# Half-length filter products in level 0 of a two-level convolution and adapter kernel

## The reference, cut to what matters

```
x = x + ffn0(cond0(x, style))
x = x + ffn1(cond1(x, style))
```

## Time and profile before

| | |
|---|---|
| median of 3 runs | 991.29 us (990.24 to 991.54) |
| profiled execution | 990.33 us, span 988.8 us |
| TensorE (PE) | 940.2 us busy, 95%, 4636 matmuls |
| VectorE (DVE) | 558.3 us, 56% |
| ScalarE (ACT) | 376.2 us, 38% |
| GpSimd (POOL) | 111.0 us, 11% |
| chain that ended last | PE 88%, DVE 8%, issue 2% |

### The profile page before, as it was taken

One profiled execution on the slowest core, in us unless ns is written; L12 is line 12 of the kernel. 1 busy time (PEld: TensorE's weight loads), 2 busy tenths in 40 slices (PEclk: granted clock), 3 DMA queues, 4 the chain that ended last, 5 costly groups with the idle time before them and its releaser, 6 DMA issues.

```text
span 988.8 us, 14065 instructions
## 1 busy us (share of the span) xinstructions
PE 940.2 (95%) x4636; PEld 792.4 (80%) x4636; DVE 558.3 (56%) x1133; ACT 376.2 (38%) x717; POOL 111.0 (11%) x141
## 2 busy tenths in 40 slices
PE   5899999999999999999999998839999999999997
PEld 4777888888888888888888887638888888888886
DVE  8894353353353354344344333966677767777774
ACT  2672243243243243233233221434554445444541
POOL 7100000000000000000000000710112111211121
PEclk8799999999999999999999999859999999999999
DMA  8701011011011011101101101331221222112211
GB/s 281 244 5 65 22 42 64 21 42 64 21 42 64 25 39 64 40 25 63 42 28 57 42 21 54 54 106 29 100 85 64 65 96 94 64 64 87 96 50 64
DMA packets 33567, 64.12 MB, mean 65 GB/s; under 512 B 12304, under 2 KB 13968, under 8 KB 33552
## 3 DMA queue, kind: packets, MB, share of 16 engines
q1 hardware_dynamic: 24480, 30.90, 10.6%
q0 software_dynamic: 9072, 33.03, 9.2%
HBM read 47.14 MB, written 16.78 MB: 65 GB/s over the span
## 4 chain that ended last, share of the span: by engine, by line
PE 88%; DVE 8%; issue 2%; ACT 1%; DMA 1%; POOL 0%; SPq 0%; POOLq 0%; DVEq 0%; ACTq 0%
PE conv_ps L172 9%; PE conv_ps L174 8%; PE conv_ps L173 8%; PE fold_ps L581 6%; PE prod_ps L743 6%; PE prod_ps L744 6%; PE prod_ps L745 6%; PE prod_ps L725 6%; PE prod_ps L726 6%; PE prod_ps L727 6%; PE prod_ps L824 6%; PE prod_ps L823 6%; PE fold_ps L548 3%; PE turn_ps L682 3%; PE turn_ps L704 1%
## 5 line engine op out<-in xcount | busy, mean ns | idle before, releaser
L158 DVE TENSOR_TENSOR h_lo<-conv_ps,h_hi 64x512 fp32r<-64x512 f32 x128 | 88.2, 689 | 47.3 <-ACT h_hi L637 46.4
L172 PE MATMUL conv_ps<-h_hi,e_hi 128*128 128x512 f32 x256 | 104.9, 410 | 2.4 <-issue 2.4
L657 ACT ACTIVATE cond<-conv_ps,bias,demod_tab 128x510 f32<-128x510 f32 x64 | 49.9, 779 | 144.7 <-PE conv_ps L174 132.7
L173 PE MATMUL conv_ps<-h_lo,e_hi 128*128 128x512 f32 x256 | 102.2, 399 | 0.0
L174 PE MATMUL conv_ps<-h_hi,e_lo 128*128 128x512 f32 x256 | 102.1, 399 | 0.0
L743 PE MATMUL prod_ps<-b_hi,xt 128*128 128x512 f32 x256 | 99.9, 390 | 2.3 <-DVE xt L158 2.3
L823 PE MATMUL prod_ps<-quant,xt_hi 128*128 128x512 f32 x256 | 100.3, 392 | 1.4 <-DVE xt_lo L158 1.4
L801 DVE SCALAR_TENSOR_TENSOR res<-prod_ps,norm,res 128x512 f32<-128x512 f32 x32 | 23.9, 750 | 137.3 <-PE prod_ps L745 137.3
L726 PE MATMUL prod_ps<-a_lo,xt 128*128 128x512 f32 x256 | 101.0, 395 | 0.0
L725 PE MATMUL prod_ps<-a_hi,xt 128*128 128x512 f32 x256 | 101.0, 394 | 0.0
L727 PE MATMUL prod_ps<-a_hi,xt 128*128 128x512 f32 x256 | 101.0, 394 | 0.0
(11 more groups left out here) (222 smaller groups left out, 1982.4 us busy)
## 6 DMA issues: line engine op xcount, KB each, us to landing
x_in<-in_x SPq DMA_DIRECT2D x64, 128.0 KB, 2.7
res<-in_x POOLq DMA_DIRECT2D x16, 512.0 KB, 3.6
x_after_first<-res POOLq DMA_DIRECT2D x16, 512.0 KB, 2.9
x_in<-x_after_first SPq DMA_DIRECT2D x64, 128.0 KB, 2.7
res<-x_after_first POOLq DMA_DIRECT2D x16, 512.0 KB, 3.5
out_x<-res POOLq DMA_DIRECT2D x15, 512.0 KB, 2.9
a_raw<-in_adapter_in SPq DMA_DIRECT2D x8, 512.0 KB, 8.1
b_raw<-in_adapter_out SPq DMA_DIRECT2D x8, 512.0 KB, 8.0
```

Source lines behind the costliest of these rows:

```text
L158: return nc.vector.tensor_tensor(out, whole, hi.bitcast(F32), ALU.subtract)
L172: nc.tensor.matmul(out, hi(w), moving_hi(i), start=(i == 0), stop=False)
L173: nc.tensor.matmul(out, hi(w), moving_lo(i), start=False, stop=False)
```

## The change

In level 0 the filter products are made by a scheme with three products of half length in place of four of full length. Layer 1's result is split by column parity into two halves, `CENTRE` and `ODD` (each `T2 = 256` columns, with a pad). VectorE forms differences, `BEFORE = ODD - CENTRE` and `AFTER = ODD (one column on) - CENTRE`; the sums of neighbouring filter tiles are two more tiles (4 and 5). TensorE makes a middle part (sum tiles by `CENTRE`, in `fold_ps[a]`) and two outer parts (in the halves of `conv_ps[a]`), 18 matmuls of 256 columns in all. ScalarE scales the middle; VectorE joins it with both outer parts (`dve_join`); ScalarE writes the two edge columns afterwards (`act_ends`). Level 1 keeps the four products (`pe_second_cond` and its like), but the taps' order is reversed so that layer 1's high and low parts are one 128-partition instruction each.

```
         def act_layer1(act, c, a, bufs):
-            nc.scalar.activation(ps[:, :], ps[:, :], ACT.Identity, bias=..., scale=...).then_inc(S.layer1_scaled, 1)
-            nc.scalar.activation(hi[0:C, 1:H + 1], ps[0:C, :], ACT.Identity)
-            nc.scalar.activation(hi[C:P, 2:H + 2], ps[C:P, :], ACT.Identity).then_inc(S.layer1_hi, 1)
+            for first, parity in ((CENTRE, 0), (ODD + 1, 1)):
+                last = nc.scalar.activation(data[:, first:first + T2], by_parity[:, parity, :], ACT.Identity, bias=..., scale=...)
+            last.then_inc(S.layer1_scaled, 1)
+        def dve_differences(v, c, a, bufs):
+            v.wait_ge(S.layer1_scaled, 2 * c + a + 1)
+            nc.vector.tensor_tensor(data[:, BEFORE:BEFORE + SPAN], data[:, ODD:ODD + SPAN], centre, ALU.subtract)
+            nc.vector.tensor_tensor(data[:, AFTER:AFTER + SPAN], data[:, ODD + 1:ODD + 1 + SPAN], centre, ALU.subtract).then_inc(S.differences, 1)
+        def act_layer1_hi(act, c, a, bufs):
+            act.wait_ge(S.differences, 2 * c + a + 1)
+            nc.scalar.activation(bufs.h_hi[a][:, :], bufs.data[a][:, 0:3 * SPAN], ACT.Identity).then_inc(S.layer1_hi, 1)
+        def dve_layer1(v, c, a, bufs):
+            v.wait_ge(S.layer1_hi, 2 * c + a + 1)
+            low(bufs.h_lo[a][:, :], bufs.data[a][:, 0:3 * SPAN], bufs.h_hi[a][:, :]).then_inc(S.layer1_ready, 1)
+        def pe_cond(pe, c, a, bufs):
+            part(fold_ps[a][:, 0:T2], (5, 4), CENTRE).then_inc(S.middle_done, 1)
+            part(conv_ps[a][:, 0:T2], (3, 1), BEFORE)
+            part(conv_ps[a][:, T2:H], (2, 0), AFTER).then_inc(S.cond_done, 1)
+        def act_middle(act, c, a, bufs):     # [128, 256] from fold_ps[a], scaled and biased
+        def dve_join(v, c, a, bufs):
+            v.wait_ge(S.cond_done, 2 * c + a + 1)
+            v.wait_ge(S.middle_scaled, 2 * c + a + 1)
+            nc.vector.scalar_tensor_tensor(out=out, in0=both, scalar=..., in1=middle, op0=ALU.mult, op1=ALU.add).then_inc(S.joined, 1)
+        def act_ends(act, c, a, bufs):       # after S.joined and edges: two [64, 2] copies, then cond_ready
```

The filter is first copied whole, in fp32 (`whole`, which shares its memory with the fold's inputs), and then split in one instruction of 1536 columns on each engine:

```
         def act_fold2(act, c, bufs, first=False):
+            nc.scalar.activation(flat(whole[:, 0:E_PAIRS, :, 0:C]), blocks, ACT.Identity)
+            nc.scalar.activation(flat(whole[C:P, 0:E_PAIRS, :, C:P]), blocks[0:C, :, :], ACT.Identity)
+            nc.scalar.activation(flat(whole[0:C, 0:E_PAIRS - 1, :, C:P]), blocks[C:P, 2:2 * E_PAIRS, :], ACT.Identity)
+            nc.scalar.activation(whole[0:C, E_PAIRS - 1, :, C:P], spread[0:C, 0:3:2, :], ACT.Identity).then_inc(S.fold2_whole, 1)
+        def dve_sum_taps(v, c, bufs):        # [128, 512]: tiles 4 and 5
+        def act_taps(act, c, bufs, first=False):   # high part, 1536 columns
+        def dve_taps(v, c, bufs):            # low part, 1536 columns, then fold2_ready
```

The raw x shares memory with its low part (`x_raw`, `x_lo`), and the loads wait for layer 1:

```
+                if not isinstance(c, int) or c:
+                    sp.wait_ge(S.layer1_done, 2 * c + a - 1)
+                sp.dma_start(conv.x_raw[a][0:C, :], rows[:, 0:H + 1]).then_inc(done, 16)
...
             with sp.Fori(1, NPAIR - 1) as i:
-                sp.wait_ge(S.xin_split, 2 * i + 2)
```

`x`, and the DRAM array between the levels, have two pad columns per phase. Level 1's head, taps, w1, f3 and w2 (before: issued after the b blocks) are now issued after the last hidden product of level 0, in one queue with the others and a second copy of the packed int4 matrix rolled by one row (`rolled`, 512 KB). Between the levels, TensorE does both samples' filter products ahead of the edge layers:

```
             inner_tensor(pe, 1, set1, 1)
+            for a in range(2):
+                pe_second_cond(pe, NPAIR, a, buf1)
             pe.wait_ge(S.x1_ready, 2 * NPAIR + 1)
-            for layer in range(3):
+            for layer in range(4):
                 edge_tensor(pe, 1, set1, layer)
-            pe_cond(pe, NPAIR, 0, buf1)
-            edge_tensor(pe, 1, set1, 3)
-            pe_cond(pe, NPAIR, 1, buf1)
             pe.wait_ge(S.quant_ready, KT)
```

More of the change, by code:

```diff
@@ L429, in edge_tensor @@
                     one = lambda w: (lambda i: w[3][:, side, i, :])
-                    last = products(prod_ps[1][:, side * B:(side + 1) * B], (2 + side, 1 + side, side), windows(s.down_hi), windows(s.down_lo), one(s.edge_hi), one(s.edge_lo))
+                    last = products(prod_ps[1][:, side * B:(side + 1) * B], (1 - side, 2 - side, 3 - side), windows(s.down_hi), windows(s.down_lo), one(s.edge_hi), one(s.edge_lo))
             last.then_inc(S.edge_done, 1)
@@ L580, in pe_fold2 @@
                 for i, (w, r) in enumerate(((fold2_hi, bufs.r_hi), (fold2_hi, bufs.r_lo), (fold2_lo, bufs.r_hi))):
-                    last = nc.tensor.matmul(out, windows(w)(tile), r[:, m:R_PAIRS:2, :, :], start=(n == 0 and i == 0),
+                    last = nc.tensor.matmul(out, windows(w)(4 - tile), r[:, m:R_PAIRS:2, :, :], start=(n == 0 and i == 0),
                                             stop=(n == len(FOLD2) - 1 and i == 2), skip_group_check=True)
@@ L632, in act_layer1 @@
             act.nop(nofuse=True)
-            ps, hi = conv_ps[a], bufs.h_hi[a]
+            data = bufs.data[a]
+            by_parity = conv_ps[a][:, :].rearrange("p (t two) -> p two t", two=2)
+            for first, parity in ((CENTRE, 0), (ODD + 1, 1)):
+                last = nc.scalar.activation(data[:, first:first + T2], by_parity[:, parity, :], ACT.Identity, bias=at(bias1, c, a, bufs),
+                                            scale=at(scale1, c, a, bufs))
+            last.then_inc(S.layer1_scaled, 1)
@@ new lines, in dve_layer1 @@
+        def dve_layer1(v, c, a, bufs):
+            v.wait_ge(S.layer1_hi, 2 * c + a + 1)
+            low(bufs.h_lo[a][:, :], bufs.data[a][:, 0:3 * SPAN], bufs.h_hi[a][:, :]).then_inc(S.layer1_ready, 1)
+        def pe_cond(pe, c, a, bufs):
+            if a == 0:
+                pe.wait_ge(S.fold2_ready, c + 1)
+            pe.wait_ge(S.layer1_ready, 2 * c + a + 1)
+            cut = lambda w, first: (lambda u: w[a][:, first + u:first + u + T2])
+            part = lambda out, filters, data: products(out, filters, tiles(bufs.e_hi[:, :, a, :]), tiles(bufs.e_lo[:, :, a, :]),
+                                                       cut(bufs.h_hi, data), cut(bufs.h_lo, data))
+            part(fold_ps[a][:, 0:T2], (5, 4), CENTRE).then_inc(S.middle_done, 1)
+            part(conv_ps[a][:, 0:T2], (3, 1), BEFORE)
+            part(conv_ps[a][:, T2:H], (2, 0), AFTER).then_inc(S.cond_done, 1)
@@ L888, in program @@
         buf1 = level_buffers(conv, 1)
+        setup_inputs(level1, 1, set1)
         setup_late(level1, 1, set1)
         setup_early(level1, 1, set1)
[L891 removed]
+        packed, rolled, nibble = T1("packed", [P, D], I32), T1("rolled", [P, D], I32), [T1(f"nibble{i}", [P, D], I32) for i in range(2)]
         buf1.sums, buf1.neg_sum = T1("sums", [P, 2]), T1("neg_sum", [P, 1])
@@ L1152, in edge_tiles, with middles, ends @@
                 tile_hi(L, s, "down")
-            def ready(L):
+            def middles(L, c, bufs):
                 act.wait_ge(S.bias4_ready, L + 1)
+                for a in range(2):
+                    act_middle(act, c, a, bufs)
+            def ends(L, c, bufs):
                 act.wait_ge(S.edges_done, L + 1)
+                for a in range(2):
+                    act_ends(act, c, a, bufs)
             nc.scalar.preload_act_table(ACT.Sqrt)
@@ L1183, in first_step @@
                 act_layer1(act, c, 0, buf0)
-                act_fold3(act, c, buf0)
                 act_layer1(act, c, 1, buf0)
+                for a in range(2):
+                    act_layer1_hi(act, c, a, buf0)
+                act_fold2(act, c, buf0)
                 act_scores(act, i, buf0)
+                act_taps(act, c, buf0)
+                act_exp(act, i, buf0)
                 if first:
                     act_b(act, 0, 3)
-                act_exp(act, i, buf0)
-                act_fold2(act, c, buf0)
+                if not last:
+                    act_fold_start(act, c + 1, buf0)
                 if first:
@@ L1193, in first_step @@
                 act_gated_turn(act, i, buf0)
-                act_cond(act, c, 0, buf0)
-                act_cond(act, c, 1, buf0)
+                for a in range(2):
+                    act_middle(act, c, a, buf0)
+                for a in range(2):
+                    act_ends(act, c, a, buf0)
             first_step(0, True)
-            with act.Fori(1, NPAIR - 1) as i:
+            with act.Fori(1, NPAIR - 2) as i:
                 first_step(i, False)
+            first_step(NPAIR - 2, False, True)
             f = NPAIR - 1
@@ L1236, in _ @@
             v.sem_inc(S.scored, 1)
-            for a in range(2):
-                nc.vector.memset(x_in[a][0:C, H:H + 1], 0.0)
-                nc.vector.memset(x_in[a][C:P, 0:1], 0.0)
             def split(c, bufs, first=False):
```

318 lines of the change are left out of this document (202 added, 116 removed).

## The result

The changed kernel takes 1006.79 us, median of four runs (1005.05 to 1012.3), against 991.08 for the kernel before (four runs, 990.24 to 991.54): a ratio of 1.0169, 95% interval [1.0129, 1.0209]. It is 15.7 us slower; the forecast was 994.9 and its range ended at 1002.

A forecast was written before the change was run, and what follows sets the result against it. Level 0 and level 1 were taken as TensorE streams at full clock. -14.1 (steps) + 15.6 (head) + 2.6 (passage) = +4.1 made 990.33 into 994.4 profiled, median 994.9; own range 991 to 999, with rivals and bounds 985 to 1002.

The forecast's parts named there:

- the mechanism at the scores: Level-0 step: TensorE waits 0.34 for the turned activations and restarts for 0.12, 0.46 us a step lost; bounds 0 and 0.7.
- Steps of level 0: Fourteen steady steps, 1 to 14: 14 x (1.47 - 0.46) = 14.1 us gained; bounds 9 and 20.6.
- The mis-sized term: Level-0 filter products: 2.80 us a sample becomes 2.06, at 0.114 a product; gain 1.47 us a step.
- the lower bound (0.122): Level-0 filter products priced at 0.122 us each, as if first starts were spread over the block: gain 1.20 a step.
- The spares of 0.35 to 0.4: Level-0 step: margins at the adapter's output (0.35), filters' low parts (0.4) and second gate (0.4), so no further wait.
- third rival: Level-0 steps: a spare is gone and TensorE stops a second time, 14 x 0.4 and more, 1000 us; chance 0.20.
- Head and step 0: Before step 1: VectorE is the queue and step 1 moves from 86.67 to 102.3; 15.6 us lost, bounds 11 and 19.7.
- The walk through the queues: Head and step 0: old durations through the new order; first filter product 41.9, fold3 56.6, routing 74, VectorE until 91.1.
- second rival: Head loses less: TensorE keeps 2.4 GHz or VectorE's waits overlap; 11 us there, 1 between levels, 988.2; chance 0.18.
- Passage with the first step: Between the levels: later first edge, shorter edge chain, half rate in the loop's first 3 to 6 us; 2.6 lost, bounds 0 and 4.5.
- Level 1: Level 1's own loop keeps its products, order and full TensorE: nothing, within 1 us.

The follow-up runs named there:

- second profile: The changed kernel run once more, unaltered: 1007.29 us (1005.47 to 1009.41); the profiled execution took 1006.3 us, span 1004.7.
- fold3_late: Changed kernel with fold3 back behind both samples' layer 1 and fold2 between the halves of the first hidden product: 999.99 us.
- first profile: The profiled execution among the changed kernel's own four runs, nothing altered, the slowest of them: 1012.3 us, span 1010.7.
- streamed: combined with VectorE's output-weight low parts placed where it idles, ScalarE's conversions moved ahead, TensorE taking blocks in the order made: 983.80 us.
- combined: Changed kernel with fold3_late's order, step 1's fold input and four weight blocks ahead of the head's joins, and edges_first's order: 994.50 us.
- streamed_edges_last: streamed with the change's passage between levels: filter products ahead of the four edge layers, nibble conversions behind the conversions of their results: 988.84 us.
- edges_first: Changed kernel with the earlier order between levels: edge layers 0 to 2, first filter products, edge layer 3, second; nibble conversions first: 1001.22 us.
- streamed_filled: streamed with 58 products of 256 columns whose results nobody reads, ahead of the first filter products: 983.63 us.

## Why the prediction was wrong

The direction was right (slower had 0.50), and so was the mechanism at the scores, but the size was more than four times too small: +3.6 forecast, +15.7 measured. Against the second profile, step by step:

- **Steps of level 0: -14.1 forecast, -9.8.** The scores' term was right to the hundredth (0.34 + 0.12, and `fold3_late` gives back 0.46). The mis-sized term is the filter products': 2.80 + 2.87 became 2.15 + 2.23, a gain of 1.29 a step and not 1.47. They start 0.119 apart, near the price of the lower bound (0.122), not 0.114 as fold2's did before; fold2's own are 0.119 apart in the changed kernel. The rest is 0.13 a step, mostly in the hidden products: the restart behind the score sum now falls on a product of 512 columns where fold2 (256) took it. The spares of 0.35 to 0.4 held, all three; the third rival's mechanism did not occur.
- **Head and step 0: +15.6 forecast, +19.0 (21.9 in the first profile), bound 19.7.** The walk through the queues was good: first filter product 42.97 (41.9 predicted), first a block 51.83 (51.3), fold3 57.42 (56.6), routing 75.00 (74), output product 92.10 (91.1). The step that failed is the clock at its end: I let the 48 output products run at full rate after a wait of 4 us, 11.0 as at 75.66, and they took 13.5. That is 2.5 of the 3.4. In the first profile the half rate lasted through both samples' filter products as well, another 3.0. The second rival (a lighter head) lost; its ground, that the clock had stayed up after 2.29 at 75.66, did not carry over to 4.06.
- **What I did not see in the head** is how much of it was order. The queue was taken as it stood, and `streamed` takes 12.4 off `combined`'s 17.6 (10.7 by the times) with the order of the weight blocks alone, on all three engines.
- **Passage with the first step: +2.6 forecast, +1.7 (3.4 in the first profile, 4.6 in `streamed_edges_last`).** Right within its bounds, and for the reason given: half rate in the loop's first step.
- **Level 1: "nothing, within 1", +4.7.** This step failed. A step takes 20.09, not 19.91, which is 2.6 over the fourteen further steps; the matrix products start 0.233 apart, not 0.229, and fold2's 0.120, not 0.115. Level 0's fold2 widened too (0.114 to 0.119), so it may be the same thing that mis-sized the filter products. Two shifts in memory gave back at most 0.04 a step, 80 more instructions on TensorE nothing; its cause stays open. The other 2.0 is the last step: TensorE waits 1.10, not 0.67, for the ends, now two instructions a sample and not one, and then 16 products took 5.4, not 3.8 (in `edges_first`, `combined` and `streamed_edges_last` they stayed at 3.8). Before, and in the second profile:

```profile
974.60 0.75 PE L682 MATMUL turn_ps<-ident,cond 128*128 128x128 f32 x4 [0.67 <-ACT cond L661]
...
988.93 0.75 PE L792 MATMUL turn_ps<-ident,cond 128*128 128x128 f32 x4 [1.10 <-ACT cond L722]
```

- **The last step of level 0** had no term; it gave +0.4, or +1.7 to 1.9 where 24 output products caught 1.2 GHz after its two waits of 1.6. Which of the two an execution gets looks like chance: `streamed` has +0.2 and `streamed_filled`, with the same step, +1.9.

The sum of what was missed is 4.3 + 3.4 + 4.7 - 0.9 + 0.4, or 11.8 before rounding, which is the 15.9 of the profile less the 4.1 forecast. The range was too narrow because level 1 had only 1 us in it and the clock after the last wait nothing, and because the steps and the head came out near or beyond their worst bounds together: the terms' own worst bounds (-9, +19.7, +4.5, +1) add up to 1006.5, beyond the 1002 given.

## What to carry to other kernels

A change of the steady step that lengthens a chain in the prologue is priced by walking the queues, but first ask whether the queue's order is still the right one: here reordering turned +15.7 into -7.4 us. After a wait of TensorE count the half rate of what may follow, not the wait alone, and give it its own bounds: in these traces the clock stayed up after 2.29 us, fell after 2.72 and 4.06, and after two waits of 1.6 it fell in some executions and not in others. Put TensorE work that is free to move directly ahead of a loop, not ahead of a chain of small waits.

## What the runs showed that I had not expected

- Beside GpSimd's 1024-column subtractions, VectorE's subtractions of two SBUF inputs take about that length more: 0.42 became 2.6 us and 1.22 became 3.4, and moving 9 us of VectorE work to an idle GpSimd cost 6 us.
- Fillers keep TensorE's clock only where they reach up to the work: 26 with 3.76 us idle behind them saved the filter products about 1 us, 50 with 0.88 kept them all at full rate. In no kernel here did they shorten the time.
- Two profiles of one program differed by 6.0 us: 3.0 in the head and 1.5 in the last step of level 0, where the longer one spent more time at 1.2 GHz, and 1.7 in the passage, where both had 30.7 us at 1.2 GHz but at other places. The times of the changed kernel scatter by 7 us, those of the kernel before by 6, those of `streamed` by 2.
